# One attention kernel, two ways to get the probabilities to the value product: turned by TensorE after the exponential, or made transposed from the start

## What is computed

```python
x = x + attention(layernorm(x))        # 16 heads of 64, rotary q and k, causal
x = x + memory_attention(layernorm(x), ctx)   # a 16-head memory matrix per batch, scanned over 64 context rows
x = x + experts(layernorm(x))          # router, top 2 of 8 experts, silu(gate) * up, down

# the attention, per batch and head
scores = q @ k.T / 8                    # 1024 x 1024, only keys <= query
weights = softmax(scores)
out = weights @ v                       # then concatenated heads @ W_out
```

## Time and profile before

| | |
|---|---|
| median of 3 runs | 2758.88 us |
| the profiled execution | 2762.53 us |
| its span, first to last instruction | 2760.8 us |
| TensorE, weight loads, VectorE, ScalarE, GpSimd busy | 95%, 84%, 72%, 59%, 54% |
| mean granted TensorE clock | 0.983 |
| context stage | 0 to 37 us |
| attention stage | 37 to 1547 us |
| memory phase | 1547 to about 2034 us |
| expert phase | about 2034 us to the end |

### The profile page before, as it was taken

One profiled execution on the slowest core, in us unless ns is written; L12 is line 12 of the kernel. 1 busy time (PEld: TensorE's weight loads), 2 busy tenths in 40 slices (PEclk: granted clock), 3 DMA queues, 4 the chain that ended last, 5 costly groups with the idle time before them and its releaser, 6 DMA issues. The chain is left out here.

```text
span 2760.8 us, 51135 instructions
## 1 busy us (share of the span) xinstructions
PE 2616.1 (95%) x16935; PEld 2321.7 (84%) x16935; DVE 1994.0 (72%) x4219; ACT 1622.4 (59%) x3158; POOL 1502.3 (54%) x1677
## 2 busy tenths in 40 slices
PE   7999999999999999999997799999969999999997
PEld 5888888888888888888886588888769999999997
DVE  6777787777777777777777688988756666666665
ACT  3666676666666666666666433333336666666665
POOL 3676757676757676677662444444434444444444
PEclk9999999999999999999999799999979999999999
DMA  6654454444544444444436465555344443444433
GB/s 172 121 130 106 109 127 112 114 117 108 137 101 112 112 119 114 118 98 105 96 82 155 107 190 147 161 147 142 104 133 106 101 106 54 107 107 103 103 58 49
DMA packets 192751, 316.69 MB, mean 115 GB/s; under 512 B 60496, under 2 KB 106224, under 8 KB 189488
## 3 DMA queue, kind: packets, MB, share of 16 engines
q1 hardware_dynamic: 149472, 218.43, 32.2%
q0 software_dynamic: 43088, 95.88, 14.1%
HBM read 241.08 MB, written 75.17 MB: 115 GB/s over the span
## 5 line engine op out<-in xcount | busy, mean ns | idle before, releaser
L1206 ACT ACTIVATE a_pt<-a_PT 128x512 fp32r<-128x512 f32 (+3 forms) x768 | 349.6, 490 | 408.3 <-PE a_PT L1065 401.0
L1353 DVE TENSOR_TENSOR a_pt<-a_PT,a_pt 128x512 fp32r<-128x512 f32 (+3 forms) x768 | 401.1, 550 | 151.0 <-ACT a_pt L1206 147.6
L1343 DVE CUSTOM_DVE_ANT_0 a_S<-a_S,a_mask 128x1024 f32<-128x1024 f32 (+7 forms) x512 | 387.1, 756 | 55.5 <-PE a_S L1054 54.1
L1195 ACT ACTIVATE a_pb<-a_S,a_nmax 128x1024 f32<-128x1024 f32 (+7 forms) x512 | 379.8, 742 | 30.4 <-DVE a_nmax L1343 28.9
L1065 PE MATMUL a_PT<-early_ident,a_pb 128*128 128x128 f32 x2304 | 338.9, 274 | 37.2 <-DVE a_pt L1353 36.6
L1082 PE MATMUL a_O<-a_pt,a_v 128*128 128x256 f32 (+1 forms) x2560 | 343.3, 281 | 24.6 <-DVE a_ot L1369 17.2
L1082 PEld LDWEIGHTS a_O<-a_pt,a_v 128*128 128x128 f32 x2560 | 326.0, 191 | 38.6 <-DVE a_ot L1369 19.3
L1065 PEld LDWEIGHTS a_PT<-early_ident,a_pb 128*128 128x128 f32 x2304 | 271.9, 141 | 92.7 <-issue 56.0
L2250 POOL DMA_INDIRECT early_stage<-in_we,e_ix x119 | 134.9, 1133 | 272.7 <-issue 146.7
L1053 PE MATMUL a_S<-a_kh,a_qs 128*128 128x512 f32 (+3 forms) x768 | 278.6, 363 | 0.5 <-ACT a_pb L1195 0.5
L1054 PE MATMUL a_S<-a_kl,a_qs 128*128 128x512 f32 (+3 forms) x768 | 256.9, 347 | 0.0
(11 more groups left out here) (331 smaller groups left out, 7552.8 us busy)
## 6 DMA issues: line engine op xcount, KB each, us to landing
a_qs<-early_rot SPq DMA_DIRECT2D x256, 128.0 KB, 2.4
a_kh<-early_rot SPq DMA_DIRECT2D x256, 128.0 KB, 2.7
a_kl<-early_rot SPq DMA_DIRECT2D x256, 128.0 KB, 2.4
m_hn<-scr_hs SPq DMA_DIRECT2D x40, 516.0 KB
scr_attT<-a_ot SPq DMA_DIRECT2D x256, 64.0 KB, 2.1
early_stage<-in_wqk POOLq DMA_DIRECT2D x31, 512.0 KB, 3.9
m_att<-scr_attT SPq DMA_DIRECT2D x30, 512.0 KB, 4.6
m_rb<-scr_rinv SPq DMA_DIRECT2D x60, 256.0 KB, 5.7
```

Of the source, the lines that this page charges most:

```text
L1195: act.activation(pb[u % 2][:, 0:cols], S[u % 2][:, 0:cols], ACT.Exp, bias=nmax[:, u % GU:u % GU + 1], scale=-1.0, accum_out=rsum[:, b % 2, ...
L1206: act.activation(pt[u % 2][:, 0, 4 * s:4 * s + m, (qt % 2) * P:(qt % 2 + 1) * P], PT[(k + s) % 2][:, 0:m * P].rearrange("p (k q) -> p k q" ...
L1343: dve.tensor_tensor_reduce(out=sc, in0=sc, in1=mask[:, T - cols:T], scale=-1.0, scalar=-MASKED, op0=ALU.add, op1=ALU.min, accum_out=nmax[: ...
L1353: dve.tensor_tensor(pt[u % 2][:, 1, 4 * s:4 * s + m, q], PT[(k + s) % 2][:, 0:m * P].rearrange("p (k q) -> p k q", k=m), pt[u % 2][:, 0, 4 ...
```

## The change

In the attention stage:

- `scores` makes one matmul per chunk (`qs` x `kh`, which leaves out `kl`) and serves only the row maxima; `rowmax` puts them as columns of `nmax`.
- `turn_max`, twice per head, transposes those columns into `S[1]`; VectorE's `max_rows` spreads them over rows 64 to 71 of `qm`, a copy of the query's high part whose rows carry, for each query tile, minus its maxima, while rows 64 to 71 of `kl` are ones.
- `scoresT(n)`: 10 *slots* per head, each two key tiles x up to two query tiles of a pair. Scores are made transposed: the key tile is the weights, the queries move (256 or 128 columns), once with `kh` x `qs` and once with `kl` (72 rows) x `qm`, which also subtracts the maximum. The result is in `ST`, two banks.
- `causal` (VectorE) masks the diagonal blocks in PSUM; `exps` reads `ST` and writes `pf` (SBUF); `part_high` and `part_low` read `pf`, so that `part_low` has both inputs in SBUF. No block is turned, there are no row sums on ScalarE.
- `values`: the transposed probabilities (128 keys x 128 queries) are the weights, the value tile with 130 columns is moving (low 64, a zero; high 64, a one that makes the row sum). Per head 72 matmuls.
- Outputs are stored not turned, with the sum as column 65, to `att`; `stack(hg + 1)` is issued in unit 5 of head `hg`, after the transposed scores of head `hg - 1` are done, and has 12 DMAs as before.

In the memory phase a tile is loaded with one DMA, scaled with inverted sums, and then turned on TensorE: 8 more transposes for each of 30 tiles (`turn("a")`, `turn("b")`), in three rotating banks; the first two tiles are turned at the end of the attention stage. In the expert phase the last of the 39 blocks is peeled off the loop, so that it prepares no 40th, and the scratch for GpSimd's DMA descriptors goes from the default to 8192 bytes.

```diff
+        SLOT_AT = (5, 6, 6, 7, 8, 9, 10, 10, 11, 12)
+        TURN = (8, 9, 11, 13)
+        LATE = 7
...
                 if hg >= 2:
-                    sp.wait_ge(s_sfull, QT * (hg - 1))
+                    sp.wait_ge(s_st, NS * (hg - 1))
...
+                    row = slice(r * 32, r * 32 + 32)
+                    half = slice(r % 2 * 32, r % 2 * 32 + 32)
+                    other = slice(HD + r % 2 * 32, HD + r % 2 * 32 + 32)
+                    q = rot[sl * 32:sl * 32 + 32, r, :].bitcast(F32)
+                    k = rot[64 + sl * 32:64 + sl * 32 + 32, r, :].bitcast(F32)
+                    sp.dma_start(qs[row, sl, :].bitcast(F32), q).then_inc(s_stack[sl], 16)
+                    if r < 2:
+                        sp.dma_start(qm[row, sl, :].bitcast(F32), q).then_inc(s_stack[sl], 16)
+                        for at in (half, other):
+                            sp.dma_start(kh[at, sl, :].bitcast(F32), k).then_inc(s_stack[sl], 16)
+                    else:
+                        sp.dma_start(kl[half, sl, :].bitcast(F32), k).then_inc(s_stack[sl], 16)
 
...
-                if u % (2 * QT) in (0, QT + 2) and 0 < u < U - QT:
-                    stack(u // QT + 1)
+                if u % QT == 5 and u // QT + 1 < NG * GH:
+                    if u // QT >= 1:
+                        stack(u // QT + 1)
...
-                q = qs[:, sl, qt * P:(qt + 1) * P]
+                    pe.wait_ge(s_nb, u - 1)
+                if max_turn(u - 1) is not None:
+                    pe.wait_ge(s_m, max_turn(u - 1) + 1)
                 cols = (qt + 1) * P
                 for c0 in range(0, cols, 512):
                     c1 = min(cols, c0 + 512)
-                    out = S[u % 2][:, c0:c1]
-                    pe.matmul(out, q, kh[:, sl, c0:c1], start=True, stop=False)
-                    mm = pe.matmul(out, q, kl[:, sl, c0:c1], start=False, stop=True)
+                    mm = pe.matmul(S[u % 2][:, c0:c1], qs[:, sl, qt * P:(qt + 1) * P], kh[:, sl, c0:c1],
+                                   start=True, stop=True)
                 mm.then_inc(s_sfull, 1)
 
-            def turn(u):
-                qt = tile_of(u)
-                k = pt_index(u)
...
+            def turn_max(c):
+                hg, half = c // 2, c % 2
+                pe.wait_ge(s_nb, hg * QT + 4 * half + 4)
+                pe.wait_ge(s_m, c)
+                rows = HD + 4 * (half + 1)
+                pe.transpose(mT[0:rows, :], nmax[:, hg % 2, 0:rows], ident[:, :]).then_inc(s_mt, 1)
+            def bank_ready(kind, n):
+                k = bi[kind, n]
+                if k >= 2:
+                    kind, n = banks[k - 2]
+                    pe.wait_ge(s_exp if kind == "slot" else s_xs, n + 1)
+            def scoresT(n):
+                hg, j, s = slot_of(n)
+                sl, pr = hg % 2, PAIRS[j]
+                bank_ready("slot", n)
+                if n % NS in (0, OFF[2]):
+                    pe.wait_ge(s_m, 2 * hg + 1 + j // 2)
+                for x in range(2):
+                    kt = 2 * s + x
+                    q = slice((2 * pr + (x if s == pr else 0)) * P, (2 * pr + 2) * P)
+                    out = stbank("slot", n)[:, x * 256:x * 256 + q.stop - q.start]
+                    pe.matmul(out, kh[:, sl, kt * P:(kt + 1) * P], qs[:, sl, q], start=True, stop=False)
+                    mm = pe.matmul(out, kl[0:KM, sl, kt * P:(kt + 1) * P], qm[0:KM, sl, q], start=False, stop=True)
+                mm.then_inc(s_st, 1)
...
             def values(k):
                 hg, j = k // (QT // 2), k % (QT // 2)
                 n, h = hg // GH, hg % GH
-                done = pt_index(hg * QT + TURN[j] - 2)
+                pr = PAIRS[j]
                 if k:
                     pe.wait_ge(s_ofree, k)
                 if k % (GU // 2) == 0:
                     pe.wait_ge(s_zfree, zi[("v", n, 3)] + 1)
-                nk = 2 * PAIRS[j] + 2
-                for part, ready in ((0, s_pthi), (1, s_ptlo)):
-                    pe.wait_ge(ready, done)
-                    for kt in range(nk):
-                        c0 = P if kt == nk - 1 else 0
-                        mm = pe.matmul(O[:, c0:2 * P], v2[:, n % 2, kt, h, :, :].rearrange("p a d -> p (a d)"),
-                                       pt[j % 2][:, part, kt, c0:2 * P],
-                                       start=kt == 0 and part == 0, stop=kt == nk - 1 and part == 1)
+                for q in range(2):
+                    nk = 2 * pr + 1 + q
+                    for part, ready in ((0, s_pthi), (1, s_ptlo)):
+                        if q == 0:
+                            pe.wait_ge(ready, pair_slots(k))
+                        for kt in range(nk):
+                            c0 = 0 if kt == 2 * pr + 1 else q * P
+                            mm = pe.matmul(O[:, q * VW:(q + 1) * VW], pt[j % 2][:, part, kt, c0:c0 + P],
+                                           v2[:, n % 2, kt, h, :], start=kt == 0 and part == 0,
+                                           stop=kt == nk - 1 and part == 1)
                 mm.then_inc(s_pv, 1)
 
-            def turn_tile(u, m, a):
-
...
+            def exps(n):
+                if n in lasts:
+                    act.wait_ge(s_masked, lasts[n] + 1)
+                act.wait_ge(s_st, n + 1)
+                if n >= 3:
+                    act.wait_ge(s_ptlo, n - 2)
+                act.activation(pf[:, n % 3, 0:columns(n)], stbank("slot", n)[:, 0:columns(n)],
+                               ACT.Exp).then_inc(s_exp, 1)
+
+            def part_high(n):
+                hg, j, s = slot_of(n)
+                k = hg * len(NB) + j
+                if s == 0 and k >= 2:
+                    act.wait_ge(s_pv, k - 1)
+                act.wait_ge(s_exp, n + 1)
+                act.activation(pt[j % 2][:, 0, 2 * s:2 * s + 2, :].rearrange("p k q -> p (k q)")[:, 0:columns(n)],
+                               pf[:, n % 3, 0:columns(n)], ACT.Copy).then_inc(s_pthi, 1)
...
+            def max_rows(c):
+                hg, half = c // 2, c % 2
+                dve.wait_ge(s_mt, c + 1)
+                rows = slice(HD, HD + 4 * (half + 1))
+                pairs = (slice(0, 4, 3), slice(1, 3))[half]
+                shape = [4 * (half + 1), 2, 2, P]
+                dve.tensor_tensor(qm[rows, hg % 2, :].rearrange("r (a t i) -> r a t i", a=4, t=2)[:, pairs],
+                                  mT[rows, :].unsqueeze(1).unsqueeze(1).broadcast_to(shape),
+                                  delta[rows, :].rearrange("r (a t) -> r a t", a=4)[:, pairs].unsqueeze(3)
+                                  .broadcast_to(shape), ALU.mult).then_inc(s_m, 1)
+            def causal(n):
+                dve.wait_ge(s_st, n + 1)
+                at = stbank("slot", n)[:, :].rearrange("p (x c) -> p x c", x=2)[:, :, 0:P]
+                dve.tensor_tensor(at, at, maskT[:, :].unsqueeze(1).broadcast_to([P, 2, P]),
+                                  ALU.add).then_inc(s_masked, 1)
+            def part_low(n):
+                hg, j, s = slot_of(n)
+                dve.wait_ge(s_pthi, n + 1)
+                hi, lo = (pt[j % 2][:, a, 2 * s:2 * s + 2, :].rearrange("p k q -> p (k q)")[:, 0:columns(n)]
+                          for a in range(2))
+                dve.tensor_tensor(lo, pf[:, n % 3, 0:columns(n)], hi.bitcast(F32),
+                                  ALU.subtract).then_inc(s_ptlo, 1)
 
             def out_add(k):
                 dve.wait_ge(s_otmp, k + 1)
...
+                for n in slots_at(u - 1):
+                    part_low(n)
+                if max_turn(u) is not None:
+                    max_rows(max_turn(u))
...
+                if max_turn(u) is not None:
+                    turn_max(max_turn(u))
+                if tile_in(u, 9) is not None:
+                    turn_tile(tile_in(u, 9))
+                for n in slots_at(u):
+                    scoresT(n)
                 fill(u, 1)
                 if values_turn(u) is not None and values_turn(u) % 2 == 0:
-                    values_at(u, values_turn(u))
...
+            if here(r, i + 1) and after(r, i + 1, 2):
+                turn("a", -1, att[:, (i + 1) % 2, 0:D], "an")
...
+            if here(r, i + 1) and after(r, i + 1, 2):
+                turn("b", -1, att[:, (i + 1) % 2, D:2 * D], "an")
...
-    nc = bacc.Bacc("TRN2", target_bir_lowering=False, num_devices=1)
+    nc = bacc.Bacc("TRN2", target_bir_lowering=False, num_devices=1,
+                   dynamic_dma_scratch_size=8192)
```

More of the change, by code:

```diff
@@ L2235, in sync @@
             load_rows(j + 1)
-        sp.wait_ge(s["rows"], 16 * (NBLK + 1))
+        for t in range(RT):
+            sp.wait_ge(s[f"st{t}"], 16 * NBLK)
     def pool(gp):
```

558 lines of the change are left out of this document (291 added, 267 removed).

## The result

The changed kernel takes 3363.9 us (median of 4 runs, 3359.32 to 3377.76), the kernel before 2759.57 (4 runs): a ratio of 1.2198, 95% interval 1.2167 to 1.223. That is 604 us more where 289 were forecast.

The account below looks back on a forecast made before the run. TensorE at its upper clock level was taken as the bound. Profiled 2762.5 us + 256 (attention, +4.0 per head) + 8 (edges) + 26 (memory phase) - 2 (experts) = 3050.5, stated as 3048 us, range 2895 to 3190.

Parts of the forecast that it names:

- The sign: Whole kernel: the change was forecast to make it slower, with chance .92 (faster .06, same .02).
- TensorE's sum: Attention, TensorE's work per head counted by matmul steps: 23.4 us after the change, 2.0 more than before.
- the value matmul: Attention value product: 72 matmuls per head at 0.11 us each, set by weight load, 7.9 us per head.
- The stack: Attention: 12 DMAs issued late take 9.6 us, so TensorE waits about 1.8 us at each head's first scores.
- The step that failed: Attention, masked slots: of 1.1 us per head of waits between VectorE and ScalarE, 0.7 was added to the cycle.
- The upper bound: Attention, masked slots: at most 1.5 us per head of VectorE and ScalarE waits reach TensorE, including one lock wait.
- The clock: Attention: a granted clock under 1.00, which the waits could cause, was named as possible but not counted on.
- VectorE: Attention: VectorE has 23.3 us per head after the change, under the cycle of 26.9, so it is hidden.
- locks: Attention: part_low with two SBUF inputs waits for GpSimd's port lock, 3.7 us per head more on VectorE.
- the second rival: Attention: VectorE becomes the bound because every part_low waits, 29 us per head, 3181 us in all; chance .11.
- The edges: End and start of attention: late last values, 16 front transposes and buffers to clear, +8 us together (0 to 12).
- the experts: Expert phase: peeling the last block saves its preparation of a 40th, -2 us (0 to -6).

Follow-up runs that it names:

- cols66: Changed kernel with the value matmuls of the probabilities' low part moving only the value's high part, 66 of 130 columns: 3386.95 us.
- ls_warm_half: ls_warm without the 36 value matmuls per head for the probabilities' low part: 3157.13 us.
- ls_warm: later_split plus unused matmuls of 256 columns ahead of the value products (5, 2, 2, 8 in a head): 3184.07 us.
- split_stack: Changed kernel with the qm and kl DMAs issued last and awaited separately, at the first transposed scores: 3350.07 us.
- later: Changed kernel with the value product of each head's third pair made one unit later: 3374.38 us.
- later_split: Changed kernel with both edits, the third pair's later value product and the separately awaited qm and kl DMAs: 3236.33 us.
- before_late_stack: Kernel before the change with only the stack issued as late as in the change, the rotation not moved: 2983.26 us against 2760.07.

## Why the prediction was wrong

The sign and several terms held; the size did not, and 3363.9 lies outside the range of 2895 to 3190.

- **TensorE's sum**, 23.4 us: its largest new term held, the value matmul is 0.110 us and not set by its columns (cols66). The figure of the Trainium skill (TensorE: Matmul & The Clock Gate, Back-to-back issue gap), 81 ns at 128 columns, does not show in this stream of 130 and of 66. But that the sum stands on the path was wrong for most of it: ls_warm_half, tried on ls_warm. The +2.0 per head was added as if TensorE were still the bound.
- **The stack**: the wait was forecast at 1.8 us per head at a head's first scores and is 0.7 there. In the kernel after most of it is hidden behind the value product's lag: alone it is worth 14 us (split_stack), with that lag moved away 138 (later to later_split), the two together 128. The mechanism was forecast rightly, its place in a sum was not.
- **The step that failed** is "How much of it reaches TensorE no row shows: the bounds are 0 and [...] 1.5; I take the middle, 0.7." Measured are 3.1 us per head of waits at the value product, with ScalarE standing 10.6 at the mask. I had counted the gaps of VectorE behind each mask, and not followed the chain mask, exponential, copy, subtraction, value product, copy, addition, and back, in which every engine keeps its order. The upper bound did not bound anything, since it was worked out on VectorE's side alone.
- **The clock** is the second term that failed. Named under what would prove the forecast wrong as something "which I do not count on", so put at nothing, it fell to 0.89 and cost up to 3.3 us per head more, as much as the waits. before_late_stack went from 0.99 to 0.94 with the same matmuls.
- **VectorE**: locks as forecast in kind, 2.2 us per head for 3.7; VectorE is not the bound as a sum (21.5 us busy per head, 67%, for the forecast 23.3), so the second rival's mechanism is not what happened, though its place is part of the ring.
- **The edges**: 42 us from the last scores to the experts where 26 + 8 were forecast, with a clock of 0.93 in that stretch for 0.95; the experts 0 for -2.

Of the 9.0 us per head more, the views give: waits 3.1 (4.1 less 1.0), work 2.0 by the steps, low clock up to 3.3 (3.5 less 0.2); 0.6 or more is left that no view here names. Since the stage is a ring, these are places where the time lies, not costs that could be taken away one by one.

## What to carry to other kernels

When every engine works in its own order and a step goes around all of them within a unit, price the change along that ring and not by engine sums: list for the longest latency chain who waits for whom, and ask what each wait does to TensorE's clock. An edit that takes a wait away should be tried together with the wait that lies behind it, since here each alone showed next to nothing. A test of one part of a change has to take along what the change did to make that part possible: before_late_stack left the rotation in place, and so measured a wait that the change doesn't have. And a stage that kept TensorE 96% busy has a second asset that the sums don't show, its clock of 1.00.

## What the runs showed that I had not expected

- Useless matmuls in the waits made a kernel faster (3236 to 3184 us), with the clock of the attention stage going from 0.89 to 0.97.
- Moving half as many columns in half of the value matmuls made it slower (+23 us), with the clock going from 0.89 to 0.85; why is open.
- One VectorE and one ScalarE instruction of each value product placed some instructions later cost 338 us.
